# AdaLN block with gated delta-rule attention and an expert layer: a new order at the borders between the front's steps, the solve cut 17 + 13, and the gates of two more quarters computed in the front's last steps

## What is computed

```
h = layernorm(x) * (1 + ca) + sa
x = x + ga * attention(h)
h = layernorm(x) * (1 + cb) + sb
x = x + gb * experts(h)          # 16 experts, each takes its 32 best tokens of a sequence

attention(h), 8 heads of 16, chunks of 32 tokens:
q, k, v = silu(causal_conv4(h @ Wq)), ...      beta = sigmoid(h @ Wb)
attn    = -(k*beta) @ k.T, strictly lower; for i in 1..31: attn[i,:i] += attn[i] @ attn[:, :i]
u, w    = (attn + 1) @ (v*beta), (attn + 1) @ (k*beta)
each chunk in order: u' = u - w @ S;  o = q @ S + tril(q @ k.T) @ u';  S = S + k.T @ u'
fus     = gelu(h @ W1 + b1) @ W2 + b2;  floor = 0.2 * sigmoid(h @ floor_W + floor_b)
p       = sigmoid(fus[3]) * (1 - floor);  ctx = softmax(fus[0:3]) * (1 - p)
out     = (ctx0*fir3(v) + ctx1*fir31(v) + ctx2*o + p*v), normed twice per head, @ Wo
```

## Time and profile before

| | us |
|---|---|
| median of 3 timed runs | 993.07 |
| lowest and highest of them | 993.06, 1003.61 |
| the profiled execution, its own time | 1000.62 |
| its span, first to last instruction | 998.6 |
| busy in the span: PE, DVE, ACT, POOL | 799.1, 760.6, 430.7, 157.4 |

### The profile page before, as it was taken

The page is one execution under the profiler, slowest core; times in us unless marked ns, Lnnn a source line. Parts: engine busy times, 40 slices in busy tenths (PEclk is TensorE's granted clock), DMA queues, the critical chain, the costliest instruction groups (busy, mean ns, idle before and its releaser), DMA issues. The chain is left out here.

```text
span 998.6 us, 43330 instructions
## 1 busy us (share of the span) xinstructions
PE 799.1 (80%) x19441; PEld 502.9 (50%) x19441; DVE 760.6 (76%) x1664; ACT 430.7 (43%) x840; POOL 157.4 (16%) x212
## 2 busy tenths in 40 slices
PE   3898899989989899999855465697987641999982
PEld 2344465555555555655555465554543300666782
DVE  6255999888999888999998835889898637677641
ACT  4577555455556564544421021366756621211100
POOL 2100101001001000000000000011111104777752
PEclk9999999999999999999987666699899765999996
DMA  4410101111110100101000003954545231344477
GB/s 117 74 33 23 34 25 41 43 38 39 37 52 30 40 26 30 42 30 42 25 31 5 22 18 100 287 134 109 136 108 142 59 93 26 101 116 124 66 177 182
DMA packets 96913, 71.25 MB, mean 71 GB/s; under 512 B 18216, under 2 KB 83416, under 8 KB 96728
## 3 DMA queue, kind: packets, MB, share of 16 engines
q1 hardware_dynamic: 88536, 61.40, 21.8%
q0 software_dynamic: 6080, 6.04, 3.6%
q10 hardware_dynamic: 2112, 1.05, 0.4%
HBM read 39.99 MB, written 28.46 MB: 69 GB/s over the span
## 5 line engine op out<-in xcount | busy, mean ns | idle before, releaser
L733 PE MATMUL ps_p<-hT,Wconv 128*128 128x512 f32 x384 | 192.2, 629 | 7.4 <-PEq L114 7.1
L841 DVE TENSOR_TENSOR f_L<-f_L,f_prod 128x60 f32<-128x60 f32 (+14 forms) x240 | 121.1, 505 | 8.3
L838 DVE TENSOR_TENSOR f_prod<-f_L 128x60 f32<-128x60 f32 (+14 forms) x240 | 118.9, 496 | 6.0
L733 PEld LDWEIGHTS ps_p<-hT,Wconv 128*128 128x128 f32 x384 | 69.9, 195 | 80.2 <-issue 74.8
L1417 POOL DMA_INDIRECT got<-xh_dram,slot_row x64 | 61.2, 956 | 52.8 <-DVEq L1556 33.6
L699 PE MATMUL ps_a<-f_TT,f_r 32*32 32x64 f32 x2048 | 40.4, 242 | 18.0 <-DVE f_r L869 11.1
L1501 ACT ACTIVATE act_g<-pe_g 128x512 f32<-128x512 f32 x32 | 17.4, 595 | 81.6 <-PE pe_g L1465 81.6
L699 PEld LDWEIGHTS ps_a<-f_TT,f_r 32*32 32x32 f32 x2048 | 37.1, 124 | 27.6 <-issue 16.0
L550 POOL TENSOR_SCALAR f_ln<-f_mv 128x4 f32<-128x4 f32 x12 | 4.1, 346 | 282.5 <-DVE f_mv L969 282.5
L1425 POOL DMA_INDIRECT out_dram<-y_slots,slot_row x28 | 44.7, 1598 | 20.9 <-DMA out_dram<-y_slots,slot_row 12.2
L1180 PE MATMUL b_ps_y<-b_v_rest,fir 32*32 32x64 f32 x768 | 42.1, 285 | 4.3 <-DMA b_v_rest<-v_tok_dram 4.3
(11 more groups left out here) (325 smaller groups left out, 1950.8 us busy)
## 6 DMA issues: line engine op xcount, KB each, us to landing
w<-in_L_ffn_w_dram SPq DMA_DIRECT2D x48, 128.0 KB, 2.5
s_tok_dram<-f_s_tok SPq DMA_DIRECT2D x16, 256.0 KB, 2.1
o_tok_dram<-f_o_tok SPq DMA_DIRECT2D x16, 256.0 KB, 2.3
b_s_in<-s_tok_dram SPq DMA_DIRECT2D x16, 256.0 KB, 2.9
b_o_in<-o_tok_dram SPq DMA_DIRECT2D x16, 256.0 KB, 3.0
b_x_in<-_attn_hidden_states_dram SPq DMA_DIRECT2D x64, 64.0 KB, 2.1
out_dram<-b_x SPq DMA_DIRECT2D x64, 64.0 KB, 1.8
xh_dram<-b_xh SPq DMA_DIRECT2D x64, 64.0 KB, 1.8
```

Of the source, the lines that this page charges most:

```text
L733: last = pe.matmul(ps[:, :], g.Wconv[:, which, tap, :], tokens(t, tap), start=(tap == 0), stop=(tap == TAPS - 1))
L838: dve.tensor_tensor(tmp, M[:, :, m + 1:, m:m + 1].broadcast_to([P, 2, rows, cols]), M[:, :, m:m + 1, 0:cols].broadcast_to([P, 2, rows, col ...
L841: dve.tensor_tensor(M[:, :, m + 1:, 0:cols], M[:, :, m + 1:, 0:cols], tmp, ALU.add).then_inc(s["solved"], 1)
```

## The change

At the border, TensorE runs the first half of the k projection ahead of the sm matmul; x is turned behind s instead of ahead of dense; ScalarE writes hT behind the state and ahead of q instead of between the o tile and the dense copy; VectorE turns sm behind the short FIR. The list of banks follows: k, sm, v, x, q, f0, f1, dense. The solve runs 17 rows in an even step and 13 in the odd one, with new cuts between the parts. The logits of quarters 1 and 2 are read from DRAM by two DMAs of 512 KB in step 12, into `hT`, which nothing uses any more; in step 14 VectorE shifts and ScalarE takes the functions of three quarters; in step 15 VectorE weighs quarter 0 ahead of r, quarter 1 behind r, quarter 2 behind u. The back loads the logits of quarter 3 alone and makes only its gates, in unit 8.

```diff
@@ -464,7 +465,7 @@
         fir_bank = lambda f: (ps_r, ps_s)[f % 2]
         bank, before, count = {}, {}, []
         for i in range(FIRST, NCH):
-            for kind, n in [("sm", unit(i + 4))] + [(x, unit(i + 5)) for x in ("k", "v", "q", "f0", "f1")] + [("x", tile(i + 5)), ("dense", unit(i + 5))]:
+            for kind, n in [("k", unit(i + 5)), ("sm", unit(i + 4)), ("v", unit(i + 5)), ("x", tile(i + 5))] + [(x, unit(i + 5)) for x in ("q", "f0", "f1", "dense")]:
                 if n is not None:
                     bank[kind, n] = len(count) % 2
                     before[kind, n] = count[-2] if len(count) > 1 else None
@@ -515,6 +516,12 @@
                 n = tile(i + 7)
                 if n is not None and n >= 2:
                     load_x(n)
+                if i == NCH - 4:
+                    need(sp, s["dense_ps"], NCH - 1)
+                    for sem in sm_out:
+                        sp.wait_ge(sem, 16 * (NCH // 2 - 2))
+                    for j in (1, 2):
+                        sp.dma_start(g.kept[j].logits.rearrange("p (t n) -> p t n", t=4), a.logits[4 * j:4 * j + 4].rearrange("t p n -> p t n")).then_inc(logits_in[j - 1], 16)
                 if unit(i) is not None:
                     need(sp, s["o_copied"], i)
                     store(a.o_tok, i, o_tok[i % 2][:, :], o_out)
 # ScalarE
@@ -643,14 +650,27 @@
                         last = act.activation(by_seq(state[i % 2][:, :])[:, :, cols], by_seq(ps_s[:, :])[:, :, cols], ACT.Copy,
                                               scale=g.pair_mask[:, n2 * DH:n2 * DH + 1])
                     last.then_inc(s["state_ready"], 1)
+                if n is not None:
+                    need(act, s["x_ps"], n)
+                    need(act, s["dense_ps"], 4 * (n // 4) - 1)
+                    need(act, s["halo_ready"], n - 4)
+                    ps = ps_p[bank["x", n]]
+                    for m in range(4):
+                        b = 4 * (n % 4) + m
+                        last = act.activation(hT[(n // 4 + 1) % 2][:, b, TAPS - 1:], ps[:, m * P:(m + 1) * P], ACT.Identity,
+                                              bias=g.mod[:, SA, b:b + 1], scale=g.mod[:, CA, b:b + 1])
+                    last.then_inc(s["h_ready"], 1)
                 if i == NCH - 2:
-                    z, zf = g.gate0, g.floor0
-                    need(act, s["shifted"], 0)
-                    act.activation(g.nq0[:, :].rearrange("p (n g) -> p n g", g=G2), g.sm0[:, :, :, 14:16].rearrange("p t b g -> p (t b) g"),
-                                   ACT.Sqrt, bias=g.eps_l2[:, :]).then_inc(s["q_root"], 1)
-                    act.activation(z[:, :, 3], z[:, :, 3], ACT.Tanh, scale=0.5)
-                    act.activation(zf[:, :], zf[:, :], ACT.Tanh, scale=0.5)
-                    act.activation(z[:, :, 0:3], z[:, :, 0:3], ACT.Exp).then_inc(s["gates_exp"], 1)
+                    for j, kept in enumerate(g.kept):
+                        if j > 0:
+                            act.wait_ge(logits_in[j - 1], 16)
+                        act.activation(kept.nq.rearrange("p (n g) -> p n g", g=G2), kept.logits.rearrange("p (n r) -> p n r", r=16)[:, :, 14:16],
+                                       ACT.Sqrt, bias=g.eps_l2[:, :]).then_inc(s["q_root"], 1)
+                    for j, kept in enumerate(g.kept):
+                        need(act, s["shifted"], j)
+                        act.activation(kept.gate[:, :, 3], kept.gate[:, :, 3], ACT.Tanh, scale=0.5)
+                        act.activation(kept.floor, kept.floor, ACT.Tanh, scale=0.5)
+                        act.activation(kept.gate[:, :, 0:3], kept.gate[:, :, 0:3], ACT.Exp).then_inc(s["gates_exp"], 1)
                 if t is not None:
...
@@ -675,16 +695,6 @@
                     if i >= 2:
                         act.wait_ge(o_out[i % 2], 16 * (i // 2))
                     take_valid(o_tok[i % 2], o_wide).then_inc(s["o_copied"], 1)
-                if n is not None:
-                    need(act, s["x_ps"], n)
-                    need(act, s["dense_ps"], 4 * (n // 4) - 1)
-                    need(act, s["halo_ready"], n - 4)
-                    ps = ps_p[bank["x", n]]
-                    for m in range(4):
-                        b = 4 * (n % 4) + m
-                        last = act.activation(hT[(n // 4 + 1) % 2][:, b, TAPS - 1:], ps[:, m * P:(m + 1) * P], ACT.Identity,
-                                              bias=g.mod[:, SA, b:b + 1], scale=g.mod[:, CA, b:b + 1])
-                    last.then_inc(s["h_ready"], 1)
 # TensorE
@@ -743,12 +753,12 @@
                     need(pe, s["state_ready"], d)
                     need(pe, s["r_ready"], d - 1)
                     per_pair(narrow(ps_r), narrow(kg_cm[d % D_KG]), narrow(state[(d - 1) % 2]), every).then_inc(s["r_ps"], 1)
+                if t is not None:
+                    project(t, "k", 1, 0)
                 if t4 is not None:
                     ps = free_bank(pe, "sm", t4)
                     need(pe, s["dense_ready"], t4)
                     pe.matmul(ps[:, :], g.spread[:, :], dense[:, :], start=True, stop=True).then_inc(s["sm_ps"], 1)
-                if t is not None:
-                    project(t, "k", 1, 0)
                 if t3 is not None:
                     need(pe, s["heads_ready"], t3)
                     need(pe, s["silu_k"], t3)
...
@@ -782,6 +792,12 @@
                     need(pe, s["state_ready"], d)
                     per_pair(narrow(ps_s), narrow(k_tok[d % D_KT]), u_pair, (lambda b: b == 0) if d == 0 else never, stop=(d == NCH - 1))\
                         .then_inc(s["s_ps"], 1)
+                if n is not None:
+                    ps = free_bank(pe, "x", n)
+                    need(pe, s["xh_ready"], n)
+                    for m in range(4):
+                        last = pe.transpose(ps[:, m * P:(m + 1) * P], xh[:, m, :], g.ident[:, :])
+                    last.then_inc(s["x_ps"], 1)
...
 # VectorE
@@ -853,26 +863,33 @@
             by_head = lambda x: x[:, :].rearrange("p (n d) -> p n d", d=DH)
             wide = lambda x: x[:, :, :].rearrange("p b g -> p (b g)").unsqueeze(2).broadcast_to([P, NI, DH])
 
+            def weigh(j):
+
+                kept = g.kept[j]
+                need(dve, s["q_root"], j)
+                then(dve.reciprocal(kept.nq, kept.nq))
+                need(dve, s["gates_exp"], j)
+                then(weigh_gates(dve, then, kept.gate, kept.floor, kept.top, kept.nq))
+
             for i in range(FIRST, NCH):
                 d, t1, t3, t4, t, n, n1 = unit(i), unit(i + 1), unit(i + 3), unit(i + 4), unit(i + 5), tile(i + 5), tile(i + 6)
-                pair, low = i // 2 + 1, 1 if i % 2 == 0 else 16
-
-                def part(lo, hi):
+                pair, low = i // 2 + 1, 1 if i % 2 == 0 else 1 + EARLY
+
+                def part(n):
 
                     if 0 <= pair < NCH // 2:
-                        solve(pair, low + lo, low + hi)
-
+                        cuts = (0, 4, 6, 11, 15, EARLY) if i % 2 == 0 else (0, 2, 4, 8, 11, C - 2 - EARLY)
+                        solve(pair, low + cuts[n], low + cuts[n + 1])
+
+                if i == NCH - 1:
+                    weigh(0)
                 if d is not None:
                     need(dve, s["r_ps"], d)
                     need(dve, s["w_ready"], d)
                     need(dve, s["u_ps"], d - 1)
                     dve.tensor_tensor(r[:, :], ps_r[:, :], w_tok[d % D_W][:, :], ALU.add).then_inc(s["r_ready"], 1)
-                if t4 is not None:
-                    need(dve, s["sm_ps"], t4)
-                    need(dve, s["beta_ready"], t4 - 2)
-                    need(dve, s["inv_step"], 2 * (t4 - 2))
-                    need(dve, s["sm_halved"], t4 - 2)
-                    dve.transpose(sm_tok[t4 % 2][:, :, :].rearrange("p b r -> p (b r)"), ps_p[bank["sm", t4]][:, :]).then_inc(s["sm_turned"], 1)
+                if i == NCH - 1:
+                    weigh(1)
                 if n is not None:
                     need(dve, s["ln_inv"], n)
                     need(dve, s["xh_ready"], n - 1)
@@ -891,6 +908,12 @@
                     if t4 >= 2:
                         dve.wait_ge(s_out[t4 % 2], 16 * (t4 // 2))
                     dve.transpose(s_tok[t4 % 2][:, :], short[:, :]).then_inc(s["s_turned"], 1)
+                if t4 is not None:
+                    need(dve, s["sm_ps"], t4)
+                    need(dve, s["beta_ready"], t4 - 2)
+                    need(dve, s["inv_step"], 2 * (t4 - 2))
+                    need(dve, s["sm_halved"], t4 - 2)
+                    dve.transpose(sm_tok[t4 % 2][:, :, :].rearrange("p b r -> p (b r)"), ps_p[bank["sm", t4]][:, :]).then_inc(s["sm_turned"], 1)
                 if t3 is not None:
                     need(dve, s["gl_ps"], t3)
                     need(dve, s["TT_ready"], t3 - 4)
@@ -932,22 +955,22 @@
                 if i == NCH - 2:
                     need(dve, s["gl_ps"], NCH - 1)
                     need(dve, s["sm_halved"], 3)
```

(34 more changed lines are left out.)

98 lines of the change are left out of this document (46 added, 52 removed).

## The result

The changed kernel takes 991.5 us (median of 20 runs, 986.5 to 997.7); the kernel before, run beside it, 996.1 us (20 runs, 991.9 to 1004.3). The ratio is 0.9945, with an interval of 0.9925 to 0.9966: 3 to 7 us faster, and not the 16 us that were forecast. The profiled execution of the kernel after took 987.3 us, span 985.6, granted clock 0.920. It is one of its faster ones, while the profiled one of before was 4.5 us above its median.

The account below looks back on a forecast made before the run. PE and DVE, both nearly full, take turns waiting; DVE becomes the front's bound. Terms -16.0 + 4.2 + 0.5 - 6.5 - 2.0 = -19.8 us; leaving out 3.5 us, 993.1 - 16.3 = 977 us, range 965 to 988.

Parts of the forecast that it names:

- Steps before 0: Front before step 0, PE's alone: a gap of about 1 us at four borders goes under k, -3.8 us.
- rival A: Filled steps: PE's wait moves to v, whose bank k's silu frees behind the turn of sm; 988 us, chance 0.11.
- Steps 0 to 6: Front's filled steps, costed by DVE's work at 61.9 us a pair: 217.1 us against 227.5, 10.4 us less.
- L749's wait on the dense copy: Border: the sm matmul's wait on ScalarE's dense copy, 16.0 us in ten waits, was to go in the filled steps.
- Steps 7 to 11, and the new waits: Front: steps 7 to 10 3.1 us shorter, step 11 2.7 us shorter, new DVE waits for attn and v +4 us.
- Front's end with the fetch: Front's last steps: weighing ahead of r in step 15 costs +4.2 us, instruction fetches delayed by the DMAs +0.5 us.
- The back: Back: unit 4 without its gates -6.5 us, unit 0 with 512 KB less ahead of v -2.0 us.
- Rival C: Back gives nothing, as PE is the bound once unit 4's pause is gone: 983 us, chance 0.12.
- signs of being right: L749 without its wait, pairs 61 to 63 us, DVE waits below 10 us, r about 5 us late, units 3, 4 equal.
- signs of being wrong: v waiting on ScalarE's L600, pairs above 64 us, PE idle before r in even steps, back units 10 us or more.
- The chances for the kernel being faster and for it being within one per cent: Whole kernel, one per cent being 9.9 us: faster than 983.1 us 0.79, within one per cent 0.16, slower 0.05.

## Why the forecast was wrong

The traces differ by 13.0 us of span. The forecast's terms, in its order:

- *Steps before 0.* Forecast -3.8, measured +8.0 at the first r (+8.7 from the dense matmul at 45 us on). **This is the step that failed:** "The steps before 0 are PE's alone: a gap of about 1 us at four borders goes under k, -3.8 us." The gaps went (3.6 us), but PE's own steps are just the ones in which a new wait can't hide, and the change made two, 9.5 us on the silus of k and v. The forecast knew the chain: it is rival A, word for word, "ScalarE's loop begins with a wait for it, and k's silu is queued behind that", and named the mark of it, a wait of v on k's silu. It priced it for the filled steps, where VectorE's own lateness covers it and only 2.2 us came up, and forgot to ask the same of the steps before 0, where VectorE turned sm 5.7 us into the last of them before (116.43 less 110.76) and turns it 8.6 us into it after (123.72 less 115.14), behind the short FIR. Its reason against the stall, "in odd steps there is no table load", is a misreading: step 5 of the kernel before has one of 1.28 us ahead of k's silu (311.80), and so has the odd step -1 after (124.98). Undone in those steps alone, the first r comes 9.7 us earlier and the runs gain some 6 us.
- *Steps 0 to 6.* Forecast 217.1 us, measured 217.10. The pair of steps as VectorE's work, 61.9 us, holds: 61.7 us in the clean pairs, 32.8 and 28.9. That it is exact is luck: the 4 us of new waits stand beside this sum and could have fallen here.
- *Steps 7 to 11, and the new waits.* Forecast -3.1, -2.7 and +4, together -1.8; measured -0.6. Steps 7 to 10 did not fall to 119.0 us but rose from 122.1 to 124.1, and step 11 gave 2.6. Steps 0 to 11 gave 11.0 us, forecast 12.2. That L749's wait on the dense copy would be gone was too much: 7.3 us of 16.0 are left. In the filled steps VectorE is the bound, and its pairs of steps came out as forecast all the same.
- *Front's end with the fetch.* Forecast +4.7, measured +4.7 (88.4 for 83.8 us). The parts were less well guessed: 2.75 us of it lie between r of step 14 and the last o (forecast 4.2), 1.9 us in steps 12 and 13, where 0.5 us stood for the fetch. That the sum is exact is luck.
- *The back.* Forecast -8.5, measured -11.0: unit 4 gave 7.2 us in place of 6.5, and units 0 to 3 gave 3.6 us in place of 2.0. TensorE's wait for v at the back's start fell from 4.3 to 2.4 us, just the half that was taken; the other 1.7 us are not explained, and in the kernels whose gates stand in the front's last steps units 0 to 3 range from 41.9 to 45.9 us (46.6 before). Rival C is out.
- *Behind the back* the traces differ by 3.7 us more, in which the change has no part. Kernels with and without the gates show either of two lengths from the last unit to VectorE's first operation in the experts' stage, 33 us or 29 to 31 us; VectorE waits there for a DMA (rows from route_dram), 13.07 us before and 10.23 after.

These sum to -13.0 us, where -19.8 were forecast, and the failed term alone is 11.8 us of it the wrong way; the back and what lies behind it hid half of that in the traces (2.5 and 3.7 us). In the timed runs they don't: the forecast's ratio was 977 / 993.1 = 0.984, the measured one 0.9945, a miss of 10.7 us, about the size of that one term. With the term put right, by the border from step 0 on, the runs give 0.988, and a rest of 4 us stays open: the gain of the filled steps may be smaller in the median execution than in the profiled ones, but no run here isolates that.

Rival A's number was met, 988 us for 993.1 x 0.9945 = 987.6, but not in its way: it had the loss in the filled steps and counted the 3.8 us before step 0 as gained. Of the signs of being right all but one came: pairs of steps of 60.8 to 62.9 us, VectorE's waits some 8 us, r some 5 us behind the turn of o, units 3 and 4 of the back equally long (9.47 us); L749's wait was not gone. Of the signs of being wrong, v's wait on k's silu came. The chances for the kernel being faster and for it being within one per cent add up to 0.78 and 0.17, not to 0.79 and 0.16.

## What to carry to other kernels

A bank's order is a list of who waits for whom: when work is reordered, write down for each tile which tile had its bank before and what stands ahead of that tile's copy in the copying engine's queue, and do it once for each regime of the pipeline, the filling steps too. A wait is free only where its engine isn't the bound; in a stretch that is one engine's alone every new wait is paid in full, and here more than in full (8.7 us for 5.9). And the order that is best in the steady state need not be used where it isn't steady: a condition on the step gave some 6 us, about as much as the whole change had.
